# The masks of the first score pass, added by VectorE while it takes the row maxima

## The reference, cut to what matters

```python
# third layer (causal): queries from x, keys and values from the context
scores = einsum('hbqd,hbkd->hbqk', Q_, K_) / d ** 0.5
scores = where(key_masks == 0.0, NEG, scores)
scores = where(tril == 0.0, NEG, scores)
attn = softmax(scores, axis=-1)
...
# fourth layer, self-attention (banded): the last W = 64 keys up to the query, with a linear bias per head
mask = (j <= i) & (i - j < W)
s = einsum('bhqd,bhkd->bhqk', q, k) / sqrt(DH) + bias
s = where(mask, s, -1e9)
a = softmax(s, axis=-1)
# then cross-attention with the context (full, no mask), and a feed-forward of 1024 columns
```

## Time and profile before

| | us |
|---|---|
| median of 3 runs (lowest, highest) | 1832.75 (1827.45, 1833.13) |
| the profiled execution, its own time | 1834.59 |
| its span, first to last instruction | 1832.5 |
| mean granted clock of TensorE in it, of full speed | 0.937 |

### The profile page before, as it was taken

One profiled execution on the slowest core, in us unless ns is written; L12 is line 12 of the kernel. 1 busy time (PEld: TensorE's weight loads), 2 busy tenths in 40 slices (PEclk: granted clock), 3 DMA queues, 4 the chain that ended last, 5 costly groups with the idle time before them and its releaser, 6 DMA issues.

```text
span 1832.5 us, 27225 instructions
## 1 busy us (share of the span) xinstructions
PE 1615.1 (88%) x9568; PEld 834.5 (46%) x9568; DVE 914.4 (50%) x2244; ACT 737.6 (40%) x1281; POOL 251.8 (14%) x116
## 2 busy tenths in 40 slices
PE   5999888888999988878999998887899999988786
PEld 2346445424435645532533554553253355545234
DVE  2653644472464474447166346445625635644561
ACT  1651434164264252417236316142724632514362
POOL 1012211201102121110110312111011031112102
PEclk9998998889999898889999989889999998988899
DMA  9001203402100211240210030224111013031300
GB/s 324 1 6 35 35 17 55 104 1 109 48 1 7 41 30 32 39 104 1 110 47 1 7 57 14 49 54 72 36 75 47 1 21 55 2 62 41 60 24 12
DMA packets 44869, 84.17 MB, mean 46 GB/s; under 512 B 10417, under 2 KB 28593, under 8 KB 44465
## 3 DMA queue, kind: packets, MB, share of 16 engines
q1 hardware_dynamic: 44288, 78.42, 18.2%
q10 hardware_dynamic: 432, 3.83, 0.5%
HBM read 42.37 MB, written 2.10 MB: 24 GB/s over the span
## 4 chain that ended last, share of the span: by engine, by line
PE 55%; issue 24%; DVE 8%; ACT 5%; POOL 4%; SPq 3%; DMA 1%; ACTq 0%; DVEq 0%; POOLq 0%
PE ring L1078 7%; PE obank L1088 7%; PE ring L1068 6%; PE ring L1029 5%; DVE nmax L912 4%; PE obank L1022 4%; PE ring L1144 3%; PE obank L1287 3%; PE ring L1327 3%; PE ring L1251 2%; SPq L381 2%; PE ring L1050 2%; ACT region_e L681 2%; PE ring L1268 2%; POOL q_all L528 2%
## 5 line engine op out<-in xcount | busy, mean ns | idle before, releaser
L912 DVE TENSOR_REDUCE nmax<-ring 128x2 f32<-128x1024 f32 (+4 forms) x384 | 318.2, 855 | 208.0 <-PE ring L1237 143.1
L681 ACT ACTIVATE region_e<-ring 128x1024 f32<-128x1024 f32 (+4 forms) x384 | 269.2, 732 | 140.9 <-PE ring L1237 87.3
L788 DVE CUSTOM_DVE_ANT_0 region_d<-ring,maskb 128x512 f32<-128x512 f32 x256 | 165.9, 687 | 101.1 <-issue 101.1
L605 ACT ACTIVATE region_e<-region_d,nmin 128x512 f32<-128x512 f32 x256 | 182.6, 714 | 81.8 <-DVE nmin L788 80.2
L673 ACT ACTIVATE q_all<-ring 2x1024 fp32r<-2x1024 bf16 x96 | 97.5, 1016 | 244.3 <-PE ring L1298 243.7
L1022 PE MATMUL obank<-cbf 128*128 128x512 bf16 x648 | 173.8, 412 | 0.0
L1237 PE MATMUL ring<-cbf 64*128 64x128 bf16 (+1 forms) x2048 | 168.2, 251 | 0.0
L1251 PE MATMUL ring<-k_tiles_a,q_all 64*128 64x512 f32 (+4 forms) x384 | 86.3, 457 | 65.5 <-DMA q_all<-q_parts 54.3
L1078 PE MATMUL ring<-region_q 64*128 64x512 f32 x512 | 126.1, 613 | 5.4 <-ACT region_q L594 5.4
L539 POOL TENSOR_TENSOR nat_x<-nat_n,rows 128x1024 f32<-128x1024 f32 x16 | 37.6, 2352 | 671.6 <-DVE nat_n L833 507.8
L1088 PE MATMUL obank<-region_e,vs 128*64 128x512 f32 x512 | 124.0, 605 | 0.0
(11 more groups left out here) (169 smaller groups left out, 2260.9 us busy)
## 6 DMA issues: line engine op xcount, KB each, us to landing
q_all<-q_parts SPq DMA_DIRECT2D x288, 64.0 KB, 2.3
k_tiles_a<-k_parts SPq DMA_DIRECT2D x144, 64.0 KB, 2.3
k_tiles_b<-k_parts SPq DMA_DIRECT2D x144, 64.0 KB, 2.3
region_b<-in_w_f SPq DMA_DIRECT2D x8, 1024.0 KB, 5.2
wvo<-in_wv SPq DMA_DIRECT2D x4, 1024.0 KB, 7.8
wqk<-in_wq SPq DMA_DIRECT2D x4, 1024.0 KB, 11.0
wqk<-in_wk SPq DMA_DIRECT2D x4, 1024.0 KB, 12.9
wvo<-in_wo SPq DMA_DIRECT2D x4, 1024.0 KB, 5.4
```

What stands on the lines that cost most here:

```text
L605: ins = act.activation(e0[:, n % E0, h, :], sm0[:, n % 2, h, :], ACT.Exp, bias=nmin0[:, n, h:h + 1], scale=-1.0, accum_out=sum0[:, n, h:h ...
L681: act.activation(e16[:, n % 4, 2 * u:2 * u + 2, 0:nq], slot((a, "B", g, kt, u))[:, :, 0:nq], ACT.Exp)\
L788: ins = dve.tensor_tensor_reduce(out=sm0[:, n % 2, h, :], in0=slot(("S0", p, kt))[:, h, :], in1=maskb[:, :], scale=-1.0, scalar=3.0e38, op ...
L912: dve.tensor_reduce(nmax[:, qt, 2 * u:2 * u + 2], slot(name)[:, :, 0:nk], AX.X, ALU.max, negate=True)\
```

## The change

The first pass no longer adds masks on TensorE, in either masked stage. In the full stage nothing changes. VectorE's `maxima` adds them for the causal and the banded stage: after a `hold()`, for each of the two heads of the job, one `tensor_tensor_reduce` adds the mask table to the scores in place in PSUM (with scale -1.0 and a minimum, as in the first attention stage) and writes the negated maximum of that head. The tables change their form with it: the causal one is now one row of 512 columns (zeros, and then the triangle) of which the last `nk` are read, the banded one 192 columns of which the last `nk` are read. The constants grow by 64 columns in all. The list of holds grows by 64 per sequence.

```diff
--- before.py
+++ after.py
@@ -54,7 +54,7 @@
         ("b1", 8), ("ga1", 2), ("be1", 2), ("g1", 2), ("b1n", 2), ("g2", 2), ("b2n", 2)]
 ROWS = [("bv0", 4), ("bo0", 1), ("bv1", 1), ("bg", 1), ("ga1", 1), ("be1", 1), ("bv2", 1), ("bo2", 1), ("sbv", 1),
         ("cbv", 1), ("b2", 1), ("g1", 1), ("b1n", 1), ("g2", 1), ("b2n", 1), ("g3", 1), ("b3n", 1)]
-CONSTS = [("ident", P), ("halves", 2 * P), ("maskA", 2 * P), ("maskB", 2 * P), ("bandA", 2 * BAND), ("bandB", 2 * BAND),
+CONSTS = [("ident", P), ("halves", 2 * P), ("maskA", S), ("maskB", 2 * P), ("bandA", BAND), ("bandB", 2 * BAND),
           ("keyrows", S), ("slopes", 2 * GROUPS), ("tri", P)]
 
 
@@ -146,7 +146,7 @@
 DVE_LINKS = 106
 ACT_LINKS = 5
 POOL_LINKS = 4
-HOLDS = UNITS0 + 5 + 3 * GROUPS
+HOLDS = UNITS0 + 5 + 3 * GROUPS + 4 * UNITS
 
 
 def build(nc, io, out):
@@ -909,8 +909,17 @@
                     _, nk = seen(a, qt)
                     name = (a, "A", g, qt, u)
                     dve.wait_ge(*filled_by(name, b))
-                    dve.tensor_reduce(nmax[:, qt, 2 * u:2 * u + 2], slot(name)[:, :, 0:nk], AX.X, ALU.max, negate=True)\
-                        .then_inc(*ends_drain(name))
+                    if a == FULL:
+                        dve.tensor_reduce(nmax[:, qt, 2 * u:2 * u + 2], slot(name)[:, :, 0:nk], AX.X, ALU.max, negate=True)\
+                            .then_inc(*ends_drain(name))
+                        return
+                    hold()
+                    table = cb("maskA", nk, at=S - nk) if a == CAUSAL else cb("bandA", nk, at=BAND - nk)
+                    for i in range(2):
+                        scores = slot(name)[:, i, 0:nk]
+                        ins = dve.tensor_tensor_reduce(out=scores, in0=scores, in1=table, scale=-1.0, scalar=3.0e38, op0=ALU.add,
+                                                       op1=ALU.min, accum_out=nmax[:, qt, 2 * u + i:2 * u + i + 1])
+                    ins.then_inc(*ends_drain(name))
 
                 def maxima_cols(a, g):
 
@@ -1249,11 +1258,7 @@
                     for i in range(2):
                         own = slice(64 * i, 64 * i + 64)
                         ins = pe.matmul(dst[:, i, 0:nk], q_tiles[g][own, u, qt * P:(qt + 1) * P], k_tiles[g][own, u, k0:k0 + nk],
-                                        start=True, stop=(a == FULL))
-                    if a == BANDED:
-                        ins = mask_heads(dst, "bandA", nk, BAND, 0, BAND - nk)
-                    elif a == CAUSAL:
-                        ins = mask_heads(dst, "maskA", P, P, nk - P, 0)
+                                        start=True, stop=True)
                     ins.then_inc(*ends_fill(name))
 
                 def pass_b(a, g, kt, u):
@@ -1399,10 +1404,10 @@
             put(name, np.tile(table[64 * half:64 * half + 64], (2, 1)), half * n)
 
     put_halves("halves", (p == x).astype(np.float32))
-    put_halves("maskA", np.where(x > p, NEG, 0.0))
+    put("maskA", np.concatenate([np.zeros((P, S - P)), np.where(x > p, NEG, 0.0)], axis=1))
     put_halves("maskB", np.where(p > x, NEG, 0.0))
     ahead = y - W - p
-    put_halves("bandA", np.where((ahead <= 0) & (ahead > -W), 0.0, NEG))
+    put("bandA", np.where((ahead <= 0) & (ahead > -W), 0.0, NEG))
     behind = y - p
     put_halves("bandB", np.where((behind >= 0) & (behind < W), 0.0, NEG))
     head_slopes = (2.0 ** (-8.0 * np.arange(1, H + 1, dtype=np.float32) / H)).astype(np.float32)
```

## The result

The changed kernel takes 1865.3 us (median; 1859.4 to 1869.8) against 1831.0 of the kernel before in the same runs: a ratio of 1.018, 95% interval [1.014, 1.021]. The forecast was 1829, range 1818 to 1845. The time lies outside the range, on the other side of the kernel before.

A forecast was written before the change was run, and what follows sets the result against it. No single bound was seen (TensorE busy 88%, VectorE 50%), so stages were priced separately: 4 x (-0.1 causal - 1.0 banded) + 0.2 constants = -4.2 us, giving 1829 us as median; range 1818 to 1845.

The forecast's parts named there:

- the price of a job: VectorE's masked first-pass jobs, causal and banded: each 0.11 us dearer, 28 us of VectorE in all.
- I take 0: VectorE's sum written back into PSUM: no extra cost, since reads from PSUM and SBUF cost the same.
- the eight starting jobs of the causal stage: First-pass jobs back to back on VectorE: 0.9 us longer, of which 0.65 lies beside an existing wait.
- The rival of the dear write: Both masked stages: the write into PSUM makes a job 0.15 us dearer, +11 us, so 1840 us; chance 0.17.
- an interval above 0.65 us: Sign that the forecast is wrong: VectorE's operations of 512 elements start more than 0.65 us apart.
- The causal stage: Start and groups of the causal stage: -0.1 us per batch in sum, with +0.9 and -0.6 as ends.
- add up and only the last drain's 0.11 remains: Second and third causal group: jobs filled 0.09 us sooner, drained 0.11 later; about -0.1 and -0.3 us.
- Causal groups that grow by more than 0.5 us: Sign that the forecast is wrong: such growth in the causal stage would mean VectorE sets the pace there.
- The clock: Rival: TensorE's clock falls more often, 14 us, so 1843 us; chance 0.20; sign: mean clock below 0.937.
- The banded stage: Second and third banded group -0.5 us each, the start 0: -1.0 us per batch, with 0 and -2.5 as ends.
- ScalarE's wait for the key tiles grew: Sign that the forecast is right: in the banded stage ScalarE waits longer for the key tiles; no size given.
- The +0.2 us for the longer constants: Before the first product: constants grow by 64 columns of 2312, on the path once, +0.2 us.

The follow-up runs named there:

- e3: The changed kernel, but VectorE's operation writes its sum to a bf16 scratch in SBUF instead of PSUM; 1.003 of the kernel before.
- e5: The changed kernel with the sum written to SBUF and four products with a table of zeros per first-pass job on TensorE; 0.999 of the kernel before.
- e1: The changed kernel (sum to PSUM) with four products with a table of zeros per first-pass job put back on TensorE; 1.010 of the kernel before.
- e2: The kernel before without first-pass masks (left out of the computation), VectorE's old reduction kept, sums of banded outputs bounded; 0.997 of the kernel before.
- e9: The changed kernel with the banded stage's mask products back, so the change is in the causal stage alone; 1.010 of the kernel before.
- e4: The kernel before plus six idle products of 512 columns per group of the full stage, in each group's second half; 0.996 of the kernel before.
- e8: The kernel before plus idle products in the full stage and first banded group, with more at the start of both stages; 1.006 of the kernel before.

## Why the prediction was wrong

**The step that failed first** is the price of a job, "I take **0.11 us a job**", and in it the term "I take 0" for the write into PSUM. Without that write the price was good: in e3 the operation has the durations of its row, one job of 512 columns follows the other after 1.23 us (1.14 before), and the eight starting jobs of the causal stage take 0.78 us more, where 0.9 was forecast. The write adds 36 ns per operation and 57 to the last read, and the starting jobs take 1.35 us more. In the time the zero was worth 1.5%, some 27 us (1.018 against 1.003). The equal prices of *reads* from PSUM and SBUF were taken for the price of a write; no row showed one. The rival of the dear write had this step nearly right (0.15 us a job), but at 1840 us it lacked what the later drains do to the clock; the sign set for it, an interval above 0.65 us, was just not reached (0.64 and 0.65). The Trainium skill had spoken against that zero (Perfetto Trace Analysis, section Optimizing Scalar/DVE Operations: overhead of about 60 ns on SBUF and 125 on PSUM). The estimate of 0.13 us a job that the prediction worked out from these figures stands beside a measured 1.43 - (0.61 + 0.61 + 0.08) = 0.13 until the result and 1.30 - 2 x 0.61 = 0.08 back to back.

**The causal stage** was forecast at -0.1 us a sequence at an unchanged clock and measured at +1.5: +0.8 between the marks, and +0.7 ahead of the first one where +0.2 was forecast (from the first starting job to the mark, in the second sequence, 651.40 to 659.26 against 644.05 to 651.21). Without the write the way to the first mark grew by 0.1 (e5), and in e3 the three groups changed by +0.06, -0.10 and -0.03 us, where +0.1, -0.1 and -0.3 were forecast; so the argument that successive shortenings "add up and only the last drain's 0.11 remains" held but for the third. With the write a later drain counts several times in a group: 0.08 to 0.13 us a job became 0.26 to 0.36 a group (e1 against e5). In the loop of the ring TensorE waits for the drain of the job three back, and two such waits are seen in the changed kernel between the third and the fourth mark (0.38 and 0.20 us, above). All in all the operation costs a group 0.5 to 0.7 us (e1), the products give back 0.1 to 0.4 (e2). "Causal groups that grow by more than 0.5 us" was named as a sign of failure; they do so only with the fall of the clock.

**The clock** was a rival (0.20, three falls in two batches, 14 us), added to a forecast that otherwise held. The sign named for it came: 0.898. The size failed: some 32 of the 35 us lie in groups that ran at the lower clock, and the time at that clock rose by 61 us in the causal and 77 in the banded stage. And the rivals were taken as cases of which one comes, each added to a forecast that holds. They act together: VectorE's later drains and TensorE's missing products empty the same stretches. With the old reduction the removal gains 0.3%, with the new operation it costs 0.4% with the sum in SBUF (0.999 to 1.003) and 0.8% in PSUM (1.010 to 1.018). The intervals of each of these two pairs overlap, but both go the same way, against the gain with the old reduction.

**The banded stage** was forecast at -1.0 us a sequence, from shorter groups at the full clock. Those groups never ran at the full clock in the changed kernel: 12.14 us in place of 9.73 in the third. What they would gain at the full clock (-0.5 each) no run shows. The Trainium skill's rule that short idle times between groups can make the clock swing (TensorE: Matmul & The Clock Gate, section A second HAM failure mode) agrees with the changed kernel's windows at 684 us (0.97 us busy of 2.00, then 0.50) and is not enough by itself, since e9 held the clock at 1.00 through the same gap.

**What was right.** The cast behind the causal start is short now (0.20 at 658.73), as the wait for GpSimd is past. In the second sequence ScalarE's wait for the key tiles grew, from 2.02 to 3.41 us, as the sign had it:

```profile
760.00 0.49 ACT L681 ACTIVATE region_e<-ring 128x384 f32<-128x384 f32 x1 [3.41 <-DMA k_tiles_b<-k_parts]
```

Over the four sequences the sign is weaker: 2.10, 2.02, 4.83 and 2.99 us before, 3.29, 3.41, 3.50 and 2.65 in the changed kernel. That a gain ahead of this wait is worth nothing is better seen in the kernel before: where its first banded group took 7.31 us and not 9.6 to 9.7, the wait was 4.83. That the wait would also take the clock of what follows was not seen. The +0.2 us for the longer constants, a term without a row, didn't come: TensorE's first product starts at 18.90 us against 18.88.

## What to carry to other kernels

An operation that must write something nobody reads should write it to SBUF: here the destination alone (in place in PSUM, or a scratch in SBUF) turned a loss of 0.3% into one of 1.8%. Where TensorE's clock moves, the products that one removes are not only cost: look in windows of 2 us at where the clock falls and whether the work behind it brings it back, and price a removal at both clocks. Two rivals that empty the same engine belong in one case with a price for both together; and a mean clock is no measure of time, since the kernel with the highest one here (0.953) was slower than the kernel before.

## What was not expected of the hardware

- VectorE's sum-and-minimum operation on 512 columns: 686 ns writing to SBUF, 722 writing in place in PSUM; the read of its accumulator 83 and 140 ns. Reading the scores from PSUM is in both.
- After one idle stretch the same group of products stayed at the lower clock for 20 us while TensorE was busy nearly all the time, and came back within some 10 us when four small products per job were added (changed kernel and e5; e3, which lacks only these products of e5, has the group at 0.50 too). More work made it faster.
- Among 25 runs of the kernel before (those beside e1 to e4), the clock went from 0.935 to 0.943 and the time with it, by some 12.6 us per 0.01 (a straight line through them; correlation -0.81). Between kernels that slope doesn't hold (e8).
